# Loading the first twenty blocks of a matrix in transfers of 1 MB instead of the first eight

## The reference

```python
def _L0_gnn_ref(x, adj_norm, kernel, bias):
    return jax.nn.relu((adj_norm @ x) @ kernel + bias)

def _L1_gnn_ref(u, v, uv_adj_mat, vu_adj_mat, ...):
    for _ in range(3):
        v = _mlp(uv_adj_mat @ u, uv_W1, uv_b1, uv_W2, uv_b2, uv_W3, uv_b3)   # three leaky-relu layers
        u = _mlp(vu_adj_mat @ v, vu_W1, vu_b1, vu_W2, vu_b2, vu_W3, vu_b3)
    return v

x = _layernorm(x + _L0_gnn_ref(x, adj, L0_gnn_kernel, L0_gnn_bias))
x = _layernorm(x + _L1_gnn_ref(x, v, adj, adj, ...))
```

## Time and profile before

| what | value |
|---|---|
| median of 3 runs | 1169.57 us (1169.35 to 1169.69) |
| the profiled execution, its own time | 1169.33 us |
| its span | 1167.5 us |
| TensorE (PE) busy | 1153.9 us, 99% of the span |
| VectorE (DVE) busy | 737.0 us, 63% |
| ScalarE (ACT) busy | 660.1 us, 57% |
| HBM read | 258.61 MB, 223 GB/s over the span |
| transfers of adj | 8 of 1 MB, 472 of 512 KB |

### The profile page before, as it was taken

How to read it: one execution, slowest core, us unless ns; L and a number is a source line. 1 busy time by engine, 2 the same in 40 slices (tenths; PEclk the granted TensorE clock), 3 DMA queues, 4 the chain that set the end, 5 groups by cost and what they waited for, 6 DMA issues and landing times.

```text
span 1167.5 us, 13724 instructions
## 1 busy us (share of the span) xinstructions
PE 1153.9 (99%) x5242; PEld 953.5 (82%) x5242; DVE 737.0 (63%) x889; ACT 660.1 (57%) x813; POOL 3.3 (0%) x8
## 2 busy tenths in 40 slices
PE   7999999999999999999999999999999999999997
PEld 6888888888888888888888888888888888887876
DVE  7997676458555555555545746553566555678984
ACT  7765555346554555555444754554556544667874
POOL 0000000000000000000000000000000000000001
PEclk9999999999999999999999999999999999999999
DMA  9988775568366646555656736555564656589871
GB/s 383 403 308 321 246 271 193 204 216 288 120 207 215 213 154 212 204 191 180 211 186 216 246 115 220 205 183 184 196 237 166 212 190 225 173 296 359 309 269 36
DMA packets 72353, 261.60 MB, mean 224 GB/s; under 512 B 8032, under 2 KB 8800, under 8 KB 71264
## 3 DMA queue, kind: packets, MB, share of 16 engines
q1 hardware_dynamic: 72144, 260.61, 63.0%
q10 hardware_dynamic: 144, 0.13, 0.0%
HBM read 258.61 MB, written 2.10 MB: 223 GB/s over the span
## 4 chain that ended last, share of the span: by engine, by line
PE 94%; DMA 3%; DVE 2%; ACT 0%; SPq 0%; issue 0%; ACTq 0%
PE agg_ps L923 28%; PE agg_ps L916 28%; PE agg_ps L909 28%; PE pre_ps L820 4%; DMA adj_raw<-in_adj 3%; PE hid_ps L781 1%; PE hid_ps L783 1%; PE hid_ps L782 1%; DVE adj_lo L761 1%; PE hid_ps L842 1%; PE hid_ps L856 0%; ACT adj_hi L628 0%; DVE stats L641 0%; SPq L490 0%; PE hid_ps L859 0%
## 5 line engine op out<-in xcount | busy, mean ns | idle before, releaser
L761 DVE TENSOR_TENSOR adj_lo<-adj_raw,adj_hi 128x1024 fp32r<-128x1024 f32 x464 | 548.1, 1221 | 224.6 <-ACT adj_hi L628 219.2
L909 PE MATMUL agg_ps<-adj_hi,feat_hi 128*128 128x512 f32 x1484 | 586.4, 395 | 7.3 <-ACT adj_hi L628 7.3
L916 PE MATMUL agg_ps<-adj_hi,feat_lo 128*128 128x512 f32 x1484 | 579.2, 390 | 0.0
L628 ACT ACTIVATE adj_hi<-adj_raw 128x1024 fp32r<-128x1024 f32 x464 | 467.6, 1051 | 82.2 <-PE agg_ps L923 69.1
L923 PE MATMUL agg_ps<-adj_lo,feat_hi 128*128 128x512 f32 x1484 | 459.0, 391 | 0.2 <-DVE adj_lo L761 0.2
L909 PEld LDWEIGHTS agg_ps<-adj_hi,feat_hi 128*128 128x128 f32 x1484 | 279.4, 188 | 65.8 <-issue 9.2
L916 PEld LDWEIGHTS agg_ps<-adj_hi,feat_lo 128*128 128x128 f32 x1484 | 279.5, 188 | 59.3 <-issue 1.9
L923 PEld LDWEIGHTS agg_ps<-adj_lo,feat_hi 128*128 128x128 f32 x1484 | 278.8, 188 | 59.9 <-DVE adj_lo L761 1.5
L522 ACT ACTIVATE hid<-hid_ps,params 128x512 f32<-128x512 f32 (+2 forms) x82 | 55.2, 673 | 61.3 <-PE hid_ps L783 50.7
L593 ACT ACTIVATE in_hi<-part 128x512 fp32r<-128x512 f32 x24 | 15.2, 634 | 110.4 <-DVE part L750 110.4
L522 ACT ACTIVATE post<-pre 128x512 f32<-128x512 f32 x39 | 24.7, 633 | 88.0 <-DVE pre L728 88.0
(11 more groups left out here) (80 smaller groups left out, 389.4 us busy)
## 6 DMA issues: line engine op xcount, KB each, us to landing
adj_raw<-in_adj SPq DMA_DIRECT2D x472, 512.0 KB, 5.6
adj_raw<-in_adj SPq DMA_DIRECT2D x8, 1024.0 KB, 8.1
resid<-in_x SPq DMA_DIRECT2D x8, 256.0 KB, 8.0
out<-resid SPq DMA_DIRECT2D x7, 256.0 KB, 5.2
params<-in_weights SPq DMA_DIRECT2D x1, 386.0 KB, 4.9
b_row<-in_bias_rows SPq DMA_DIRECT2D x1, 128.0 KB, 5.4
out<-resid SPq DMA_DIRECT2D x2, 64.0 KB, 1.7
out<-resid ACTq DMA_DIRECT2D x1, 128.0 KB, 2.0
```

The source lines that it names most:

```text
L628: act.activation(split_hi(b)[:, i * CHUNK:(i + pieces) * CHUNK], adj_raw[:, h % RAW, 0:pieces * CHUNK], ACT.Copy).then_inc(adj_hi_ready, 1)
L761: dve.tensor_tensor(split_lo(b)[:, slot], adj_raw[:, h % RAW, 0:pieces * CHUNK], split_hi(b)[:, slot].bitcast(F32), ALU.subtract).then_inc ...
L909: pe.matmul(group_bank(g), feat_hi[feats][:, tile(src, i)], split_hi(b)[:, piece(i)], start=start, stop=False)
L916: pe.matmul(group_bank(g), feat_lo[feats][:, tile(src, i)], split_hi(b)[:, piece(i)], start=False, stop=False)
```

## The change

The constant `WHOLE` is 20 instead of 8. Blocks 8 to 19 come as twelve transfers of 1 MB instead of twenty-four of 512 KB.

```diff
-WHOLE = 8
+WHOLE = 20
```

## The result

| | before | changed |
|---|---|---|
| median (22 runs each) | 1169.53 us | 1171.17 us (1170.75 to 1171.83) |
| ratio of changed to before | | 1.0015, 95% interval 1.0009 to 1.0021 |
| the profiled execution, its own time | 1169.33 us | 1171.32 us |
| its span | 1167.5 us | 1169.5 us |

The change costs 1.64 us at the median (1.05 to 2.5 us by the interval of the ratio). The forecast was +0.9 us.

A forecast was written before the change was run, and what follows sets the result against it. TensorE, busy 1153.9 of 1167.5 us, was taken as the bound. New lateness of 1.3 us at block 14 less the 0.42 lost before gave +0.9 us, so 1170.4 us (0.07% slower), range 1168.9 to 1171.7.

The forecast's parts named there:

- the bounds that the working had for its own terms: Net loss at block 14, forecast +0.9 us: least +0.8, and +1.25 with no gain of bandwidth; chance 0.62.
- a starved queue: Rival: SP's wait for two slots starves the queue, blocks 12 to 19 come slower; 1171.0 us at most, chance 0.08.
- What bounds the kernel: TensorE, busy 1153.9 of 1167.5 us; a shift of it that survives to 76 us reaches the end whole.
- Latency of the first half, 1.47 us: Both halves wait for the whole block; TensorE can begin without waiting no earlier than the landing row plus 1.47 us.
- Bytes and bandwidth, 0.06 us a block: Whole blocks land 2.50 us apart against 2.56 for two halves, so 0.06 us gained per block, counted from block 8.
- The estimate of 24 us: Skill's larger gain: 2 us a block for twelve blocks if transfers ran one at a time; the prediction rejected it.
- Block 9, 0.99 us late: TensorE could begin block 9 at 35.43 instead of 34.57: 0.86 us late, plus 0.13 after the wait.
- the faster rival: Load 19's 1.29 us delay belongs to halves and goes, with TensorE's 0.42 us of small waits: 1169.0 us, chance 0.10.
- Block 12, "just touched" at 43.96: Block 12 can begin at 43.96 against TensorE's 43.95: 0.01 us late and perhaps 0.13 again.
- Given back at 60 us: Rival: the 0.47 us wait at 60 us vanishes, net 0.4, 1169.9 us, chance 0.12; the forecast took nothing back.
- Issue and queue: Whole transfers issue later, the first half losing about 1.2 us of lead; queue stays filled, cost nothing.
- Slower by half pace: Rival: the new wait at block 9 brings back TensorE's cold pace, costing 2.5 us: 1172.9 us, chance 0.04.

## Why the prediction was right, and where it was off

The time fell into the range and the direction was right, but the loss of 1.64 us at the median is above the bounds that the working had for its own terms (+0.8 to +1.25). It stayed in the range thanks to room that was meant for other things, a starved queue and the scatter of the median, and that part is luck. Two of the signs that the prediction named as speaking against it appeared: block 9 began without a wait, and the share of the transfers fell below 1 between 35 and 55 us. Both come from things that it had taken from the old landings as fixed: the place of the fetch packet and the cost of the weights.

- **What bounds the kernel.** Right. TensorE is busy without a break from 76 us on, as before; the shift at block 14 (1.96 us) is the shift of the span (2.0 us).
- **Latency of the first half, 1.47 us.** Right to 0.02 us. In the changed kernel blocks 11 and 12 begin to be split at 39.58 and 43.50, and their second halves are begun by TensorE at 42.52 and 46.44: in both cases 2.94 us later, against the predicted 1.47+0.13+1.36 = 2.96. By itself it costs 1.28 us (the run with halves that wait for both), where the working without the gain had 1.25; some 0.2 of the 1.28 may be the bias row's.
- **Bytes and bandwidth, 0.06 us a block.** The size was right in the rows (2.50 us between whole blocks). At the end of the run it is worth about 0.26 us. The estimate of 24 us for transfers one at a time rests on the fit in the Trainium skill ("DMA: Bandwidth & Descriptors", Anatomy of one DMA), which the page gives for transfers issued by GpSimd; here SyncE issues them. With a filled queue neither the 12 larger transfers nor the 12 fewer issues returned anything near it.
- **Block 9, 0.99 us late.** It didn't wait in the profiled execution, because the instruction fetch held one engine back 3 us later than before. I had left open what made load 19 late, and gave the landings of before as fixed. This moved a wait of the same kind from block 9 to block 11; the sum did not gain by it as the faster rival had it. Behind block 11 TensorE was 42.52-1.36-39.93 = 1.23 us late, where the working had 1.22: its lateness there hangs on the landing of block 11, which came where the working had it (its split began at 39.58, against 39.87-0.24 = 39.63).
- **Block 12, "just touched" at 43.96.** This is the step that was mis-sized. It took the landing row of before, 42.79 less 0.30, which holds the weights ahead of it at the 0.35 us that they cost there. It began to be split at 43.50, 1.0 us later, and TensorE's second half of it began 1.1 us later than the 43.96+1.36 of the prediction. Moving the bias row alone takes 1.64-0.83 = 0.81 us from the loss by the medians of two sessions (0.56 within one session, against the matrix moved). What is left, +0.83, is the size of the forecast (+0.9), and in that run block 14 begins at 49.52, where "about 49.5" was predicted. That kernel is not quite the one forecast, since the 0.2 us of the row are gone from it too.
- **Given back at 60 us.** Rightly taken as nothing: 0.57 us between the same two matmuls before and after. The stretch did not shorten though TensorE came 1.96 us later.
- **Issue and queue.** Right, -0.01 us when tried alone. In the changed kernel block 12 is issued at 33.61, 3.50 us behind the landing of block 8, as the working had it.
- **Slower by half pace.** Did not come. After the waits of 0.69 and 0.54 us matmuls follow 0.23 us apart (41.09, 41.32), and the granted clock is 1.00, the level of 2.4 GHz.

- **Prices of the rivals.** By their own terms three are 0.1 to 0.2 us too low: 1169.57-0.42 = 1169.15 (not 1169.0), with the 0.47 at 60 us 1168.7 (not 1168.5), and 1169.57+0.43 = 1170.0 (not 1169.9). No chance hangs on it.

So the mechanism was right. By the medians the 1.64 us are 1.09 for the wait for both halves without the bias row, less some 0.26 for the larger transfer, and 0.81 for the bias row. The first is shown. The second and the exact size of the third are not, as they compare sessions; that the row is dear is shown. Why it costs the landing 1.4 us here and 0.35 us in the kernel before is not settled: the packets of 512 bytes that took over 100 ns were 36 of 256 after and 12 before, and none in the runs where the row stood at block 14 or 15, but in the runs with the row ahead of block 12 and that block in halves their number went from 4 to 27. It differs between executions, and only one of each kernel is recorded. No version beat the kernel before beyond what can be told.

## What to carry to other kernels

Where the consumer is nearly as fast as the transfers and the queue is full, a larger transfer saves almost nothing per byte (here 0.06 us in 2.56) and makes the consumer wait for the last byte before it may touch the first. Work that cost out with the distance of two landings (here 1.28 us) against the slack at the tightest block. A landing is set by the last of sixteen engines, so a row of landings from the old trace may only be carried over if what holds that one engine back (an instruction fetch, a small or repeated read ahead of it) stands at the same place in the queue. Small transfers that read the same bytes many times belong away from the tight stretch; here that was worth 0.6 to 0.8 us with whole blocks, and nothing in the kernel before.

## What the hardware showed that I had not expected

- One 16 KB packet of instruction fetching took 1.02 to 1.11 us, and every landing behind it was late by one engine, by 1.3 us in the kernel before, for as long as the queue was full: there until about 41 us, when at least one other engine had lost as much to the weights. It came at 31.5 to 32.2 us in nine recorded executions and at 34.3 to 35.0 in five, with halves as with whole blocks.
- A broadcast row of 512 bytes, read 128 times (64 KB), held the landing of block 12 back by 1.57 us alone, and together with the matrix by 0.35 to 1.8 us (the 1.8 with blocks 8 to 11 whole: 43.83-39.47 for the landings of blocks 12 and 11, 2.56 due). It held block 10 back by 0.7 us, and blocks 14 and 15 by 0.1 to 0.2. A matrix of the same 64 KB in as many packets of 512 bytes took 0.15.
